# One attention step in two halves: row-tiled scores beside the maxima, then full-width products, then P times V over eight key tiles

## The reference

```python
xn = _layernorm(x, axis=-1)                                  # x: (8, 1024, 256)
# attention, 16 heads of 64
q = (einsum('bnd,ed->bne', xn, Wq) + bq) ...                 # k and v alike
att = softmax(einsum('bhqd,bhkd->bhqk', q, k) / sqrt(64), axis=-1)
attn = einsum('bhqk,bhkd->bhqd', att, v) ... @ Wo.T + bo
# experts: 64 of hidden width 192, top 8 of each token, at most 128 tokens for each; one shared expert
h = silu(einsum('ecd,edf->ecf', xb, w_gate)) * einsum('ecd,edf->ecf', xb, w_up)
y = einsum('ecf,efd->ecd', h, w_down)                        # weighted and added to its tokens
return x + attn + (routed + shared)
```

## Time and profile before

| | us |
|---|---|
| median of three runs | 3608.57 (3605.85 to 3610.23) |
| the profiled execution | 3610.97 |
| its span, first to last instruction | 3609.2 |
| PE busy | 3503.0 (97%) |
| POOL busy | 2711.3 (75%) |
| DVE busy | 2517.0 (70%) |
| ACT busy | 1685.6 (47%) |

### The profile page before, as it was taken

One profiled execution on the slowest core, in us unless ns is written; L12 is line 12 of the kernel. 1 busy time (PEld: TensorE's weight loads), 2 busy tenths in 40 slices (PEclk: granted clock), 3 DMA queues, 4 the chain that ended last, 5 costly groups with the idle time before them and its releaser, 6 DMA issues. The chain is left out here.

```text
span 3609.2 us, 59812 instructions
## 1 busy us (share of the span) xinstructions
PE 3503.0 (97%) x16231; PEld 2104.9 (58%) x16232; DVE 2517.0 (70%) x3256; ACT 1685.6 (47%) x3126; POOL 2711.3 (75%) x2338
## 2 busy tenths in 40 slices
PE   8999489999999999999999999999999999999899
PEld 6888255555555555555555555555555555555487
DVE  7888467777777777777777777777777777777444
ACT  4455234444444444444444444444444444444343
POOL 1111168888888888888888889888888888889511
PEclk9999689999999999999999999999999999999899
DMA  7777545666666666666666666666666666665396
GB/s 249 230 227 224 150 117 137 173 168 168 169 168 170 170 168 168 170 171 169 170 169 172 168 169 169 171 167 171 168 171 168 168 169 172 169 172 130 117 320 227
DMA packets 393627, 635.53 MB, mean 176 GB/s; under 512 B 48048, under 2 KB 214640, under 8 KB 393584
## 3 DMA queue, kind: packets, MB, share of 16 engines
q1 hardware_dynamic: 370800, 603.54, 60.3%
q0 software_dynamic: 14336, 23.08, 3.1%
q10 hardware_dynamic: 8448, 8.39, 0.7%
HBM read 306.91 MB, written 126.12 MB: 120 GB/s over the span
## 5 line engine op out<-in xcount | busy, mean ns | idle before, releaser
L1099 DVE TENSOR_REDUCE merged<-psum 128x1 f32<-128x1024 f32 x1024 | 1206.0, 1219 | 732.9 <-PE psum L927 726.8
L1062 ACT ACTIVATE probs<-psum 128x512 f32<-128x512 f32 x2048 | 1083.3, 600 | 1160.5 <-PE psum L901 867.6
L1226 POOL TENSOR_TENSOR sums<-sums,probs 128x512 f32<-128x512 f32 x768 | 979.8, 1276 | 97.9 <-ACT probs L1062 43.4
L1227 POOL TENSOR_TENSOR sums<-sums,probs 128x512 f32<-128x512 f32 x768 | 981.1, 1277 | 0.0
L942 PE MATMUL psum<-probs,v_sb 128*64 128x512 f32 x4096 | 931.0, 596 | 0.0
L898 PE MATMUL psum<-q_full,k_full 128*128 128x512 f32 x2048 | 878.8, 429 | 0.0
L901 PE MATMUL psum<-q_rest,k_rest 65*128 65x512 f32 x2048 | 812.3, 397 | 0.0
L942 PEld LDWEIGHTS psum<-probs,v_sb 128*64 128x64 f32 x4096 | 284.0, 137 | 560.8 <-issue 498.4
L898 PEld LDWEIGHTS psum<-q_full,k_full 128*128 128x128 f32 x2048 | 388.2, 190 | 196.9 <-issue 95.2
L1127 DVE RECIPROCAL sum_all<-sum_all 128x128 f32<-128x128 f32 x512 | 448.7, 918 | 27.7 <-ACT sum_all L1070 27.7
L974 PE MATMUL psum<-x_t,w_qk 128*128 128x512 f32 x1536 | 416.3, 407 | 38.0 <-DVE w_d L1092 27.5
(11 more groups left out here) (145 smaller groups left out, 3059.8 us busy)
## 6 DMA issues: line engine op xcount, KB each, us to landing
x_t<-xt SPq DMA_DIRECT2D x118, 1024.0 KB
k_full<-high SPq DMA_DIRECT2D x256, 256.0 KB
v<-values SPq DMA_DIRECT2D x64, 512.0 KB, 3.2
w_qk<-wqk_parts SPq DMA_DIRECT2D x64, 512.0 KB
q_full<-high SPq DMA_DIRECT2D x128, 256.0 KB
q_full<-low SPq DMA_DIRECT2D x128, 256.0 KB
k_rest<-low SPq DMA_DIRECT2D x128, 256.0 KB
q_rest<-high SPq DMA_DIRECT2D x128, 256.0 KB
```

Source lines behind the costliest of these rows:

```text
L1062: nc.scalar.activation(probs[:, kt, h, :], ring[ring_place(g, j) % RING], ACT.Exp, scale=SCALE).then_inc(probs_ready, 1)
L1099: nc.vector.tensor_reduce(out=merged[:, col:col + 1], in_=work[:, 2 * h:2 * h + 2, :].rearrange("p b c -> p (b c)"), axis=AX, op=ALU.max, ...
L1226: nc.gpsimd.tensor_tensor(sums[:, half, 0, :], first[:, 0, :], probs[:, kt, 0, :], ALU.add)
L1227: nc.gpsimd.tensor_tensor(sums[:, half, 1, :], first[:, 1, :], probs[:, kt, 1, :], ALU.add).then_inc(sums_added, 1)
```

## The change

Scores no longer read rearranged copies. A key tile is now done for both heads at once: four terms (high·high, high·low, low·high, and a row with minus the maximum), each a product of 64 rows for head 0 and one for head 1, straight out of `high` and `low`, like the quads. The twelve DMAs and their four tiles go. The ring is four banks, two for each key tile, and one exponential covers both heads (128 x 1024).

The order of a step is now two halves. A half is: a quad; eight key tiles of scores with a quad behind the third, the sixth and the eighth; the full-width products; the turn of the maxima; the sums of the half before; P times V over all eight key tiles. Full-width products write into banks 0, 1 and 3 (projections, tokens) and 6 and 7 (expert). ACT copies P times V out of bank 2 (`out_copied`), and DVE divides in SBUF a step later. The gating of the expert moves from POOL to DVE. DVE's fillers move accordingly.

```diff
-SLOTS = 4
 GROUP = KT // 2
-RING = 3
-SCORES = 4 * KT
-SHUFFLES = 12
-QUADS = 4 * SLOTS
+QUADS = 8
+AFTER_PAIR = {0: 2, 1: 5, 2: 7}
...
-    ring = [psum[:, b, :] for b in range(RING)]
-    out_ps = psum[:, 3, :]
+    ring = psum[:, 0:4, :]
+    out_ps = psum[:, 2, :]
     work = psum[:, 4:8, :]
+    sum_ps, turn_ps, gu_ps, down_ps = psum[:, 4, :], psum[:, 5, :], psum[:, 6, :], psum[:, 7, :]
...
+        def quad(s, par, flags, half, q):
+            fin, att, nxt, prj = flags
+            done = 2 * QUADS * (s + 1) + 2 * (GROUP * half + q)
+            if not known(done, 1):
+                pe.wait_ge(quad_reduced, done)
...
+        def scores(s, par, flags, half, kt):
+            fin, att, nxt, prj = flags
+            t = 2 * s + half
+            if kt >= 2:
+                pe.wait_ge(probs_ready, KT * t + kt - 1)
...
+            if kt == 1 and not known(t, 1):
+                pe.wait_ge(out_copied, t)
...
+            for term in range(4):
+                if term == 3 and kt == 0:
+                    pe.wait_ge(shift_placed[half], 2 * DMA * (s + 1))
                 for h in range(2):
                     rows = slice(DK * h, DK * (h + 1))
...
+                    key, query = ((high[rows, par, 1, keys], high[rows, par, 0, cols]),
+                                  (high[rows, par, 1, keys], low[rows, par, 0, cols]),
+                                  (low[rows, par, 1, keys], high[rows, par, 0, cols]),
+                                  (first_row[rows, :], shift_row[rows, half, :]))[term]
+                    last = nc.tensor.matmul(ring[:, 2 * (kt % 2) + h, :], key, query, start=(term == 0), stop=(term == 3))
+            last.then_inc(scores_ready, 1)
...
+        def gate_up(s, par, nxt):
+            if nxt:
+                pe.wait_ge(quad_reduced, 2 * QUADS * (s + 1) + 2 * GROUP)
+            pe.wait_ge(xt_copied, s + 1)
...
         def step(s, par, flags):
             fin, att, nxt, prj = flags
...
+            for half in range(2):
+                if nxt:
+                    quad(s, par, flags, half, 0)
+                for kt in range(KT):
                     if att:
+                        scores(s, par, flags, half, kt)
+                    for q in range(1, GROUP):
+                        if nxt and kt == AFTER_PAIR[q - 1]:
+                            quad(s, par, flags, half, q)
+                if half == 0:
+                    if att:
+                        turn_tokens(s, par)
+                    if prj:
+                        project(s, par, flags, 0)
+                    if att:
+                        gate_up(s, par, nxt)
+                else:
+                    for n in range(1, 4) if prj else ():
+                        project(s, par, flags, n)
+                    if att:
+                        down(s, par, nxt)
                 if nxt:
+                    turn(s, half)
+                if (att if half else fin):
+                    add_up(2 * s + half - 1, s, half, nxt)
+                if att:
+                    pv(s, par, half)
...
+        def exp(s, half, kt):
+            t = 2 * s + half
+            act.wait_ge(scores_ready, KT * t + kt + 1)
...
+            nc.scalar.activation(probs[:, half, kt, :, :], ring[:, 2 * (kt % 2):2 * (kt % 2) + 2, :], ACT.Exp, scale=SCALE
                                  ).then_inc(probs_ready, 1)
...
-                for h in range(2):
-                    rows = slice(DK * h, DK * (h + 1))
-                    top, bottom = slice(0, DK), slice(DK, P)
-                    for dst, to, src, which in ((k_full, top, high, 1), (k_full, bottom, high, 1),
-                                                (q_full, top, high, 0), (q_full, bottom, low, 0),
-                                                (k_rest, top, low, 1)):
-                        sp.dma_start(f32(dst[to, pp, h, :]), f32(src[rows, pp, which, :])).then_inc(placed, DMA)
```

More of the change, by code:

```diff
@@ L880, in _ @@
         pe.wait_ge(set_up, 4)
[L882 to L902, removed]
@@ new lines, in turn, with turn_tokens @@
+        def turn(s, half):
+            pe.wait_ge(quad_reduced, 2 * QUADS * (s + 1) + 2 * GROUP * (half + 1))
+            nc.tensor.transpose(turn_ps[:, 0:P], merged[:, 2 * GROUP * half:2 * GROUP * half + P], ident[:]
+                                ).then_inc(turn_filled, 1)
+        def turn_tokens(s, par):
+            pe.wait_ge(probs_ready, KT * 2 * s + 7)
+            pe.wait_ge(tokens_loaded, DMA * (s + 1))
+            for kd in range(KD):
+                last = nc.tensor.transpose(ring[:, 0, kd * P:(kd + 1) * P], x_e[:, par, kd * P:(kd + 1) * P], ident[:])
+            last.then_inc(xt_filled, 1)
@@ new lines, in down, with add_up @@
+        def down(s, par, nxt):
+            if nxt:
+                pe.wait_ge(quad_reduced, 2 * QUADS * (s + 2))
+            else:
+                pe.wait_ge(y_weighted, s)
+            pe.wait_ge(hidden_ready, s + 1)
+            nc.tensor.matmul(down_ps[:, 0:D], hidden[:, 0:P], w_d0[:, par, :], start=True, stop=False)
+            nc.tensor.matmul(down_ps[:, 0:D], hidden[:, P:2 * P], w_d1[:, par, :], start=False, stop=True
+                             ).then_inc(dn_filled, 1)
+        def add_up(t, s, half, nxt):
+            if nxt:
+                pe.wait_ge(quad_reduced, 2 * QUADS * (s + 1) + 2 * GROUP * (half + 1))
+            if not known(t, 1):
+                pe.wait_ge(sum_copied, t)
+            pe.wait_ge(sums_added, 7 * (t + 1))
+            for h in range(2):
+                last = nc.tensor.matmul(sum_ps[DK * h:DK * (h + 1), :], ones[:], sums[:, 1 - half, h, :],
+                                        start=True, stop=True)
+            last.then_inc(sum_filled, 1)
@@ L1228, in step @@
                                             ).then_inc(sums_added, 1)
[L1229 to L1232 removed]
+            if nxt:
+                alone(pool, (standing, 1), (tokens_ready, s + 2))
+                nc.gpsimd.indirect_dma_start(
+                    out=x_e[:, 1 - par, :], out_offset=None, in_=io["rows"],
+                    in_offset=bass.IndirectOffsetOnAxis(ap=token[:, 1 - par:2 - par], axis=0)
+                ).then_inc(tokens_loaded, DMA)
```

558 lines of the change are left out of this document (238 added, 320 removed).

## The result

| | before | after |
|---|---|---|
| median, us | 3607.84 (3605.85 to 3610.23, 4 runs) | 3754.98 (3753.94 to 3758.24, 4 runs) |
| ratio | | 1.041 (95% interval 1.039 to 1.043) |
| span of the profiled execution | 3609.2 | 3752.2 |
| step in the loop | 45.66 | 48.17 |

The change made the kernel 4.1% slower; 3733 with a range of 3640 to 3800 was forecast. The step is the median distance from one down product to the next, 600 to 3290 us. Every execution behind this document had a mean granted clock of 0.98 to 0.99, but for one of the five of the half exponentials (0.842), whose trace isn't used.

A forecast was written before the change was run, and what follows sets the result against it. PE was taken as the bound. A step: 45.65 - 1.86 - 0.5 + 2 x 1.84 + 0.9 = 47.9 us; 62 x 2.25 = +139, head -15, together +124, giving a median of 3733 us, range 3640 to 3800.

The forecast's parts named there:

- The stalls: PE's new waits for other engines in the attention loop: 1.84 us in each half plus 0.9 once a step.
- The ring: Scores wait for an exponential to free one of two key tiles' banks: 0.40 plus 0.105 us, twice a half.
- the third quad's maxima: The fourth quad of each half waits for DVE's maxima of the quad before: 0.725 plus 0.105 us.
- gate and up: Expert products in the first half wait for the fourth quad's maxima, sharing bank 6: 0.9 us a step.
- The walk: The prediction's pass through one half of a step in time, with durations from the trace: 47.9 us a step.
- PE's own work: A loop step without any new wait: 43.3 us, from 45.65 less 1.86 and 0.5.
- The old ring's waits: In the kernel before, score loads wait for exponentials: taken as 0.5 us a step, saved by the change.
- The saved changes of shape: PE changes array shape less often in a loop step: 2.93 us before, 1.07 after, 1.86 saved.
- Rival (C): Half-height pairs in a long row don't hide their loads, 0.34 us each: 52.5 a step, about 4018; chance 0.05.
- The head: Before the loop, separate banks remove waits of projections (about 5 us) and shorten the second step (10): -15 us.
- The tail: The last two steps, with fewer products, left as they are, within 5 us.
- DMAs: Removing the twelve DMAs of a step alone is worth nothing in the loop, as PE has no wait for them.

The follow-up runs named there:

- the half exponentials: Changed kernel with each exponential covering 2 x 256 of its 2 x 512 columns, the others set once to 1: 3647.3 us, 1.011 of the kernel before.
- the turn experiment: Changed kernel with the turn of the maxima moved into the middle of P times V, four more changes of array shape a step: 3791.7 us, 1.051 of before.

## Why the prediction was right

**The stalls.** The ring, the third quad's maxima, gate and up: right in place and in kind. The walk gave 47.9 a step and 48.17 was measured, and the three waits went away with their causes, one by one and together. In size they were somewhat short. The waits come to 48.17 - 43.1 = 5.1 a step, where the walk had 4.6. Of these 0.5, some 0.35 are the exposed loads in front of the fifth and eighth key tiles, four in a step, which the walk had free. The walk priced the exponential's lag with a row of 0.11, and the first two of a step show 0.21 and 0.23.

**PE's own work.** 43.3 was forecast, about 43.1 measured (an estimate, see above). That the sum is so close is partly luck. The old ring's waits were worth 0.1 and not 0.5. Against that, half-height pairs came out at 0.23 (1510.12 to 1510.35) and not 0.235, about 0.4 over the 80 pairs of a step, and the projection that waited for maxima before was worth 0.15 that the prediction hadn't. The saved changes of shape (1.86) aren't measured by themselves. 45.66 - 43.79 = 1.87 looks like them, but holds the 0.7 of ring waits that are left; and ten changes saved at the 0.15 of the turn experiment would be 1.5. What the runs show is that such changes cost something (0.59 for four), and that the new order without its waits would be some 2.5 a step faster (43.1 against 45.66).

Rival (C), exposed loads in long rows, is wrong. Each load runs beside the pair before:

```profile
1511.04 0.40 PE L887 MATMUL psum<-high 64*128 64x512 f32 x2
1511.05 0.19 PEld L887 LDWEIGHTS psum<-low,high 64*128 64x128 f32 x2
```

The rule of the Trainium skill that led to it (TensorE: Matmul & The Clock Gate, Part 3, The mechanism), that loads overlap running matmuls only where the row group differs, isn't borne out in this trace. The Trainium skill's warning about emptying PSUM (TensorEngine Tiling, PSUM Bottleneck) fits in part: PE did wait for the engines that read PSUM, but by the latency of one round, with ACT busy 49% of the time and DVE 76%.

**The missing 22 us.** The forecast was 3733, the median 3755. From the start of the first scored step to the start of the first without projections, 62 steps, the changed kernel takes 149.8 us longer than before (452.21 to 3435.61 against 466.49 to 3300.10), where 139 was forecast: 11 us. The end adds 7.5 that were taken as zero, and the head gained 14.3 instead of 15. The last 3 lie between the profiled executions, from which I counted, and the medians. The 22 us are small against a range of 160.

**Head and tail.** The head was forecast at -15. The first scored step starts at 452.21 with a quad, and before it started at 466.49 with a score, so 14.3 earlier:

```profile
409.53 7.76 PE L912 MATMUL psum<-x_t,w_qk 128*128 128x512 f32 x24 [28.28 <-POOL first_row L1192]
418.07 0.73 PE L859 MATMUL psum<-high 64*128 64x512 f32 x4 [0.78 <-ACT high L1011]
...
452.21 0.72 PE L859 MATMUL psum<-high 64*128 64x512 f32 x4 [0.90 <-ACT minus_max L1043]
```

The kernel before:

```profile
466.49 0.79 PE L898 MATMUL psum<-q_full,k_full 128*128 128x512 f32 x1
```

The total was right and its parts were not. The prediction took 430.94 to 477.57 as the second step, but from 466.49 on these rows are the first scored step. The first 24 projections gained about 9 (8.5 us to the first quad, where the fifth projection came 18.0 behind the first), and not 5; the second step gained about 6, and not 10. The stage began 1.1 later.

The tail, taken as zero, cost 6.5: from the start of the first step without projections to the output stage it is 108.7 us, before 102.3 (the output stage adds 1.0). In that step nothing covers the maxima:

```profile
3446.86 0.44 PE L925 MATMUL psum<-ident,x_e 128*128 128x128 f32 x2
3449.37 2.93 PE L935 MATMUL psum<-x_et,w_gu 128*128 128x128 f32 x12 [2.07 <-DVE merged L1104]
```

Gate and up wait 2.07 and then run at half speed: 2.93 us instead of 1.60, at a granted clock of 0.50 (3449 to 3452), the lower level of 1.2 GHz, where it was 0.98 over the 14 us before.

**DMAs.** Worth nothing in the loop, as forecast and as measured.

## What to carry to other kernels

Grouping products of one array shape saved here something like 0.15 us for each change avoided, but it also brings steps together that hand over through other engines. Before doing it, walk one period with durations of the trace, and count for each buffer how much of PE's own work lies between filling it and needing it again. A busy share of 48% or 71% says nothing here: what counts is the latency of one round (2.45 us between quads; 2.37 from a key tile's first pair to its banks' next use, 1510.12 to 1512.49) against the work that covers it (1.84, two key tiles). A wait need not show as idle time: look also for products that last 0.50 instead of 0.39. Then ask of each wait whether it needs all that it names: one bank's number was worth 61 us, the order of two waits 23.

## What the hardware showed beyond that

- Loads behind a wait: when a pair of scores waited for a semaphore, its load was exposed, and the product lasted 0.50 instead of 0.39, so a short wait cost 0.1 us on top. A wait of almost no length still cost this 0.1 (1514.89).
- DVE's division with one operand in PSUM took 0.68 us for 128 x 512 before; with all operands in SBUF, beside a busy POOL, it takes 1.47. Of POOL's own adds those of one head (L1217) went from 1.28 to 1.35, those of the other stayed at 1.28. The cause wasn't tried. No wait of PE in the loop names this division.

```profile
L1130 DVE TENSOR_TENSOR out_raw<-out_raw,sum_all 128x512 f32<-128x512 f32 x116 | 170.6, 1471 | 0.0
```

- A score's end reached the exponential in 0.05 us when its wait came last, and in 0.12 to 0.23 when the wait for a count out of a register stood between them. In the steps that are unrolled, with the same order but counts known when the program is built, it took 0.04 to 0.05.
